# An edge-message kernel on one core: scatters eight groups behind throughout, and six slots for combined messages in place of three

## The chip, the cores and the metric

The kernel runs on one core of one Trainium2 chip. The metric is the device time of one execution in microseconds; the median of three runs of the kernel before is 1071.09 us.

## The reference

100,000 nodes with 64 features each, 25,000 edges with 32 features each. With `source, target = src, dst`:

```python
h = jnp.maximum(_layernorm(x, axis=-1), 0.0)
z = jnp.concatenate([h[source], h[target], edge_attr_32], axis=-1)
m = jax.nn.sigmoid(z @ W_f + b_f) * jax.nn.softplus(z @ W_s + b_s)
message = jax.ops.segment_sum(m, source, num_segments=100000)
mean = jnp.mean(message, axis=0)
var = jnp.mean((message - mean) ** 2, axis=0)
normed = (message - mean) * jax.lax.rsqrt(var + 1e-5) * gamma + beta
out = x + h + normed
```

## The kernel before

Stage one computes the messages. 128 edges are a tile, 4 tiles a group, and there are 49 groups (0 to 48, the last one is `LAST`). GpSimd gathers the rows of `x` for both ends of each edge by indirect DMA: 8 gathers of 128 rows for a group (line 584), into a ring of six groups. Beside each edge group a block of 16 x 128 nodes is normalised and kept as y = x + h. The engines work in steps (`step` in `vector`, `scalar` and `tensor`): in step s VectorE centres group s, TensorE transposes group s-1 and multiplies it with the weights (lines 1124, 1134 to 1138), and group s-3 is finished: VectorE forms the message, TensorE adds up the messages of edges in a group that have the same source (`combine`, lines 1164 and 1168, which signals `comb_done`), and ScalarE copies the combined messages out of PSUM (`copy_comb`, line 1036, which signals `comb_copied`). TensorE's next transposition of edge features (line 1117) waits for that copy.

The combined messages of a group stand in a slot of a ring of `COMB_SLOTS` = 3. GpSimd adds them to the table `msgs` in DRAM by four indirect DMAs with accumulation (`accumulate`, line 597, called the scatters here). A group's scatters wait for its copy, for its targets, and for the landing of the scatters of the group before (`accumulated`). Ahead of them GpSimd signals `slots_free`. For group n `copy_comb` waits for `slots_free` of n+1, and two are given at the start, so group n waits until the scatters of group n-2 have been let go.

GpSimd's order is written by hand. It gathers group n and then scatters group n-8. At n = 16, 24, 32 and 40 (`CATCH_UP`) another group's scatters stand between the first and the second half of the gathers, so that from n = 40 on GpSimd is four groups behind. Group 48 is gathered apart (`gather_last`, line 607) and is computed under the next stage. The last three groups (46 to 48, `LATE`) are not scattered in stage one: their combined messages are copied to the tile `late` and added later. Behind the scatters of group 45 GpSimd reads 12 times 128 rows of `msgs` for them (line 632, the late gathers).

Stage two scans `msgs` (25 blocks) for the sum of squares. SyncE issues its loads (line 1423) once all scatters of groups 0 to 45 have landed, the last node block is done (`y_done`, line 827) and the last transposition but one is over (`z_turned`). From the fourth block on they also wait for `cross_used`, which TensorE signals when matmuls for the joined group 47 are done (line 1150), and for the gathers of group 48. ScalarE's squares (line 1466) wait for the block and for TensorE's clearing of two PSUM banks behind those matmuls. Stage three writes out = y + normalised message.

Of the kernel before, what the change touches and what calls it, by code (L numbers as in the profile page):

```python
# [23 lines left out]
ALU = mybir.AluOpType  # L24
# [3 lines left out]
P = 128  # L28
NODES, EDGES, F, EF = 100000, 25000, 64, 32
EPS = 1e-5  # L30
TILES = 4
GATHERED = 2 * TILES
# [6 lines left out]
LAST = GROUPS - 1  # L39
# [9 lines left out]
G_SLOTS = 6  # L49
S_SLOTS = 2  # L50
E_SLOTS = 3
COMB_SLOTS = 3
LATE = 3
PRE = GROUPS - 1
EARLY = GROUPS - LATE
# [1 line left out]
SPILL = 19  # L57
KEPT_ROWS = (GROUPS - SPILL) * BULK
ACC_FIRST = 8
CATCH_UP = (16, 24, 32, 40)  # L60
ZERO_PARTS = 16
ZERO_EARLY = 5
ZERO_FIRST = 2
# [25 lines left out]
BANK_ROWS = 8  # L89
# [119 lines left out]
def build(nc, x, src, dst, ea, w_f, b_f, w_s, b_s, gamma, beta, out, msgs, y_spill):  # L209
# [7 lines left out]
    with ExitStack() as outer:  # L217
# [3 lines left out]
        def keep(name, shape, dt=F32):  # L221
            return outer.enter_context(nc.sbuf_tensor(name, shape, dt))

        at = Shared()
# [12 lines left out]
        at.late_out = keep("late_out", [P, LATE_TILES], I32)  # L237
        at.m_buf = keep("m_buf", [P, M_BUFS, S_BLK, F])
        at.m_last = keep("m_last", [P, BLOCKS[-1][1], F])
        at.sums = keep("sums", [P, 21 * F])  # L240
        at.ps_all = outer.enter_context(nc.psum_tensor("ps_all", [P, 2 * Y_ROWS, F], F32))

        at.accumulated = sem("accumulated")
# [55 lines left out]
def stage_one(nc, sem, keep, at, x, src, dst, ea, w_f, b_f, w_s, b_s, msgs, y_spill, src_rows,  # L299
# [3 lines left out]
    late_comb, late_msg, late_ids = at.late_comb, at.late_msg, at.late_ids  # L303
# [24 lines left out]
    ids = free_then(2, ALL_TILES, dt=I32)  # L328
# [4 lines left out]
    xg_last = free_last(GATHERED, F)  # L333
# [34 lines left out]
    before_scan = carver(at.sums[:, 0:BANK_ROWS * F])  # L368
    src_f = before_scan(ALL_TILES)
    msg = before_scan(TILES, F)  # L370
    comb = carver(at.sums[:, BANK_ROWS * F:20 * F])(COMB_SLOTS, TILES, F)
    sq = at.late[:, :, :]
    ids_turned = gate[:, :, :].rearrange("p (h t) f -> p h (t f)", h=2)
    upto = same[:, 0, :]
# [22 lines left out]
    def late_tiles(g):  # L397
        return slice((g.n - EARLY) * TILES, (g.n - EARLY + 1) * TILES)
# [2 lines left out]
        return late_msg[:, late_tiles(g), :] if g.late else msg[:, :, :]  # L401

    def comb_of(g):
        return late_comb[:, late_tiles(g), :] if g.late else comb[:, g.slot(COMB_SLOTS), :, :]

    def wait_slot(eng, g):

# [160 lines left out]
    def gpsimd(pool):  # L568
        pool.sem_inc(slots_free, COMB_SLOTS - 1)

        pool.memset(ident[:, :], 0.0).then_inc(masks_set, 1)
        pool.memset(upto[:, :], 1.0).then_inc(masks_set, 1)
        pool.wait_ge(masks_set, 2)
        pool.affine_select(out=ident[:, :], in_=ident[:, :], compare_op=ALU.not_equal, fill=1.0,
                           base=0, pattern=[[-1, P]], channel_multiplier=1).then_inc(masks_made, 1)
        pool.affine_select(out=upto[:, :], in_=upto[:, :], compare_op=ALU.is_ge, fill=0.0,
                           base=0, pattern=[[-1, P]], channel_multiplier=1).then_inc(masks_made, 1)

        def gather(n, tiles):
            if n >= G_SLOTS:  # L580
                pool.wait_ge(centred, n - G_SLOTS + 1)
            for j in tiles:
                for c in range(2):
                    pool.indirect_dma_start(  # L584
                        xg[:, n % G_SLOTS, 2 * j + c, :], None, x,
                        bass.IndirectOffsetOnAxis(ap=ids[:, c, n * TILES + j:n * TILES + j + 1], axis=0),
                    ).then_inc(gathered[n % G_SLOTS], 16)

        def accumulate(n):
            pool.wait_ge(comb_copied, n + 1)  # L590
            pool.wait_ge(target_done, n + 1)

            if n:
                pool.wait_ge(accumulated, 16 * TILES * n)
            pool.sem_inc(slots_free, 1)
            for j in range(TILES):
                pool.indirect_dma_start(  # L597
                    msgs, bass.IndirectOffsetOnAxis(ap=target[:, n % UNROLL, j:j + 1], axis=0),
                    comb[:, n % COMB_SLOTS, j, :], None, compute_op=ALU.add,
                ).then_inc(accumulated, 16)  # L600

        pool.wait_ge(ids_main, 32)
        behind = 0
        def gather_last(tiles):
            for j in tiles:
                for c in range(2):
                    pool.indirect_dma_start(
                        xg_last[:, 2 * j + c, :], None, x,
                        bass.IndirectOffsetOnAxis(ap=ids[:, c, LAST * TILES + j:LAST * TILES + j + 1], axis=0),
                    ).then_inc(last_gathered, 16)  # L610

        for n in range(PRE):
            gather(n, range(0, TILES // 2))
            if n in CATCH_UP:
                accumulate(behind)
                behind += 1
            gather(n, range(TILES // 2, TILES))
            if n == ACC_FIRST:
                pool.wait_ge(table_zeroed, 16 * (ZERO_PARTS + 2))
            if n >= ACC_FIRST:  # L620
                accumulate(behind)
                behind += 1
        pool.wait_ge(ids_rest, 64)
        for n in range(behind, EARLY):
            gather_last([n - behind])
            accumulate(n)
        gather_last(range(EARLY - behind, TILES))

        pool.wait_ge(late_listed, 1)
        pool.wait_ge(accumulated, 16 * TILES * EARLY)  # L630
        for t in range(LATE_TILES):
            pool.indirect_dma_start(
                was_read[:, t, :], None, msgs, bass.IndirectOffsetOnAxis(ap=late_ids[:, t:t + 1], axis=0),
            ).then_inc(late_read, 16)
# [1195 lines left out]
```

## Time and profile before

| | |
|---|---|
| median of 3 runs | 1071.09 us (1069.85 to 1071.23) |
| the profiled execution, from its first to its last instruction | 1087.2 us, 16.1 above that median |
| indirect DMAs in stage one, issued by GpSimd | 384 gathers, 184 scatters, 8 gathers of group 48, 12 late gathers |
| stage one, about | 0 to 860 us |
| scan, about | 860 to 950 us |
| output, about | 950 to 1087 us |

In a timeline each row is the start and the duration in us, the engine, the line, the operation and its tiles; in brackets stands how long the engine was idle before it, and what ended that. POOL is GpSimd, PE TensorE, PEld its weight loads, DVE VectorE, ACT ScalarE, and SPq SyncE's queue, which issues DMAs. In grouped rows "idle before" is the sum of such idle times.

### The profile page before, as it was taken

To read this page: it belongs to the slowest core of one execution; us is meant where nothing else is said; L and a number is where in the kernel's file an instruction comes from. 1 tells how busy PE (TensorE), PEld (TensorE's weight loads), DVE (VectorE), ACT (ScalarE), POOL (GpSimd) and SP (SyncE) were. 2 spreads that over 40 slices of the span, in tenths; PEclk is the share of its full clock that TensorE was granted. 3 is DMA by queue.
4 is the path that set the end of the run, shared out by engine and by line. 5 is a ranking of instruction groups with operands and counts; after the bars stand their busy time and mean duration, and the time that the engine had idled before them with its cause. 6 is when DMAs were issued, how large, how long until landed. Compare 5 with 4: busy or idle time off the path is not lost. (4 is left out here: it accounts for less than half of the span.)

```text
span 1087.2 us, 11011 instructions
## 1 busy us (share of the span) xinstructions
PE 579.7 (53%) x2442; PEld 406.6 (37%) x2442; DVE 742.1 (68%) x1551; ACT 536.9 (49%) x1185; POOL 735.4 (68%) x652
## 2 busy tenths in 40 slices
PE   0321754456553756664564556575636679844332
PEld 0121542335442534542352335454424479610000
DVE  3523766658766678757587666677566568789788
ACT  1131664556464656454565645664546556333332
POOL 7774777777878787777778777878787710650620
PEclk9855576765676565557666755655676579855555
DMA  7994443545443434434344334334333579589999
GB/s 280 416 402 151 111 124 75 123 94 123 104 120 77 125 59 79 85 56 83 62 83 78 86 53 86 62 78 82 63 76 58 153 290 410 195 254 414 416 404 387
DMA packets 88145, 176.02 MB, mean 162 GB/s; under 512 B 42561, under 2 KB 49285, under 8 KB 79663
## 3 DMA queue, kind: packets, MB, share of 16 engines
q1 hardware_dynamic: 34903, 111.46, 29.0%
q0 software_dynamic: 42880, 20.09, 16.5%
q10 hardware_dynamic: 10328, 44.12, 10.0%
q14 instruction: 26, 0.21, 0.1%
q8 instruction: 8, 0.13, 0.1%
HBM read 107.12 MB, written 68.50 MB: 162 GB/s over the span
## 5 line engine op out<-in xcount | busy, mean ns | idle before, releaser
L584 POOL DMA_INDIRECT m_buf<-in_x_dram,m_buf x384 | 368.4, 959 | 118.3 <-issue 111.6
L597 POOL DMA_INDIRECT msgs_dram<-sums,target x184 | 289.2, 1572 | 69.0 <-issue 56.0
L1164 PE MATMUL ps_all<-sums,m_last 128*128 128x64 f32 x920 | 152.2, 338 | 26.9 <-issue 23.7
L707 DVE TENSOR_REDUCE m_last<-late 128x24 f32<-128x1536 f32 (+1 forms) x49 | 85.3, 1741 | 113.8 <-ACT late L978 84.4
L1164 PEld LDWEIGHTS ps_all<-sums,m_last 128*128 128x128 f32 x920 | 145.9, 251 | 38.3 <-issue 35.4
L1117 PE MATMUL ps_all<-ident,m_last 128*128 128x128 f32 x49 | 21.2, 432 | 225.3 <-ACT sums L1036 212.0
L1138 PEld LDWEIGHTS ps_all<-m_buf 128*128 128x128 f32 x392 | 93.8, 328 | 50.0 <-issue 50.0
L1036 ACT ACTIVATE sums<-ps_all 128x256 f32<-128x256 f32 x46 | 17.6, 382 | 187.3 <-remote 187.3
L1027 ACT ACTIVATE m_last<-m_last,one_col 128x512 f32<-128x512 f32 x196 | 107.6, 550 | 1.6
L678 DVE SCALAR_TENSOR_TENSOR m_buf<-ps_all,m_buf 128x1024 f32<-128x1024 f32 x97 | 93.2, 960 | 19.3 <-remote 15.6
L827 DVE TENSOR_TENSOR y_kept<-ps_all,m_buf 128x256 f32 (+1 forms) x196 | 82.5, 422 | 26.6 <-remote 13.6
L1136 PE MATMUL ps_all<-m_buf 128*128 128x512 f32 x98 | 100.6, 1129 | 0.0
L1117 PEld LDWEIGHTS ps_all<-ident,m_last 128*128 128x128 f32 x49 | 8.9, 181 | 237.4 <-issue 237.0
L1019 ACT ACTIVATE m_last<-m_buf,m_last 128x512 f32<-128x512 f32 x196 | 93.5, 553 | 0.0
L1138 PE MATMUL ps_all<-m_buf 128*128 128x128 f32 x392 | 90.8, 411 | 0.0
L1457 ACT ACTIVATE ps_all<-y_kept 128x2048 f32<-128x2048 f32 (+3 forms) x33 | 47.0, 1432 | 80.0 <-DVE m_buf L1790 75.1
L837 DVE TENSOR_TENSOR sums<-m_buf 128x256 f32<-128x256 f32 x46 | 19.5, 423 | 95.0 <-ACT m_buf L994 86.6
L978 ACT ACTIVATE late<-m_buf 128x1536 f32<-128x1536 f32 (+1 forms) x49 | 71.5, 1459 | 25.2 <-issue 25.2
L1528 PE MATMUL ps_all<-shift_row,ones_b 3*128 3x512 bf16 x90 | 42.5, 619 | 75.1 <-ACT ps_all L1457 66.8
L809 DVE SCALAR_TENSOR_TENSOR ps_all<-m_buf,ps_all 128x512 f32<-128x512 f32 x98 | 67.7, 691 | 11.3 <-remote 8.6
L1124 PE MATMUL ps_all<-ident,m_buf 128*128 128x128 f32 x192 | 41.6, 356 | 59.2 <-issue 30.7
L687 DVE TENSOR_REDUCE ps_all<-m_buf 128x16 f32<-128x1024 f32 x49 | 59.9, 1222 | 14.0 <-DMA m_buf<-in_x_dram 12.9
(171 smaller groups left out, 1076.1 us busy)
## 6 DMA issues: line engine op xcount, KB each, us to landing
m_buf<-msgs_dram SPq DMA_DIRECT2D x38, 1024.0 KB, 8.4
m_buf<-in_x_dram SPq DMA_DIRECT2D x48, 512.0 KB
out_dram<-m_buf ACTq DMA_DIRECT2D x20, 1024.0 KB, 10.8
msgs_dram<-y_kept SPq DMA_DIRECT2D x11, 1536.0 KB
m_buf<-src_rows_dram SPq DMA_DIRECT2D x47, 256.0 KB
y_spill_dram<-y_kept ACTq DMA_DIRECT2D x19, 512.0 KB
y_kept<-y_spill_dram SPq DMA_DIRECT2D x8, 1024.0 KB, 14.8
msgs_dram<-y_kept ACTq DMA_DIRECT2D x5, 1536.0 KB
```

What stands on the lines that cost most here:

```text
L584: pool.indirect_dma_start(xg[:, n % G_SLOTS, 2 * j + c, :], None, x, bass.IndirectOffsetOnAxis(ap=ids[:, c, n * TILES + j:n * TILES + j + ...
L597: pool.indirect_dma_start(msgs, bass.IndirectOffsetOnAxis(ap=target[:, n % UNROLL, j:j + 1], axis=0), comb[:, n % COMB_SLOTS, j, :], None, ...
L678: return dve.scalar_tensor_tensor(out=xc[:, g.slot(2), rows, :], in0=row_sum[:, rows].unsqueeze(2).to_broadcast([P, n, F]), scalar=-1.0 / ...
L707: dve.tensor_reduce(row_ssq[:, rows], sq[:, rows, :], AX.X, ALU.add).then_inc(ssq_done, 1)
L809: dve.scalar_tensor_tensor(out=ps_h[:, :, :], in0=xc[:, g.slot(2), rows, :], scalar=0.0, in1=row_rstd[:, rows].unsqueeze(2).to_broadcast([ ...
L827: ins = dve.tensor_tensor(y_kept[:, bass.ds(row, n), :], ps_h[:, piece * n:(piece + 1) * n, :], xn[:, g.slot(SLOTS), of_x, :], ALU.add)
L978: act.activation(sq[:, rows, :], xc[:, g.slot(2), rows, :], ACT.Square).then_inc(squared, 1)
L1019: ins = act.activation(same_of(b, b, TILES), src_all[:, slot, b:TILES, :], ACT.Abs, scale=-1.0, bias=own[:, g.slot(UNROLL), b:b + 1])
L1027: ins = act.activation(same_of(b, b, TILES), same_of(b, b, TILES), ACT.Relu, scale=-1.0, bias=one_col[:, 0:1], accum_out=matches[:, b:b + 1])
L1136: pe.matmul(v[:, :, :], ea_t[:, :], w_e[:, :, :], start=False, stop=True, skip_group_check=True)
L1138: ins = pe.matmul(v[:, j, :], z_t[:, j, :], w_z[:, :], start=False, stop=True, skip_group_check=True)
L1164: pe.matmul(ps_c[:, j, :], same_of(b, j, j + 1)[:, 0, :], msg_of(g)[:, b, :], start=(b == 0 and not begun), stop=(b == j), skip_group_chec ...
```

## The change

GpSimd no longer catches up: it gathers group n whole and scatters group n-8, for all n up to 47. Then 6 groups (40 to 45) are left to scatter, where before 2 were (44 and 45). The 8 gathers of group 48 are spread ahead of these six, one or two each; before, two stood ahead of each of the two groups and four behind. The ring of combined messages has six slots; four lie in the tile `sums` and two in `m_buf`. With it `copy_comb` and the targets of group n wait until the scatters of group n-5 have been let go.

```diff
-COMB_SLOTS = 3
+COMB_SLOTS = 6
+COMB_FIRST = 4
-CATCH_UP = (16, 24, 32, 40)
...
-        at.sums = keep("sums", [P, 21 * F])
+        at.sums = keep("sums", [P, (BANK_ROWS + COMB_FIRST * TILES) * F])
...
-    comb = carver(at.sums[:, BANK_ROWS * F:20 * F])(COMB_SLOTS, TILES, F)
+    take_comb = carver(at.sums[:, BANK_ROWS * F:])
+    comb = [take_comb(TILES, F) if i < COMB_FIRST else free_then(TILES, F) for i in range(COMB_SLOTS)]
...
-        def gather_last(tiles):
-            for j in tiles:
-                for c in range(2):
-                    pool.indirect_dma_start(
-                        xg_last[:, 2 * j + c, :], None, x,
+        def gather_last(rows):
+            for row in rows:
+                j, c = divmod(row, 2)
+                pool.indirect_dma_start(
+                    xg_last[:, row, :], None, x,
...
         for n in range(PRE):
-            gather(n, range(0, TILES // 2))
-            if n in CATCH_UP:
-                accumulate(behind)
-                behind += 1
-            gather(n, range(TILES // 2, TILES))
+            gather(n, range(TILES))
             if n == ACC_FIRST:
                 pool.wait_ge(table_zeroed, 16 * (ZERO_PARTS + 2))
             if n >= ACC_FIRST:
                 accumulate(behind)
                 behind += 1
         pool.wait_ge(ids_rest, 64)
+        left = EARLY - behind
         for n in range(behind, EARLY):
-            gather_last([n - behind])
+            gather_last(range(GATHERED * (n - behind) // left, GATHERED * (n - behind + 1) // left))
             accumulate(n)
-        gather_last(range(EARLY - behind, TILES))
```

GpSimd's order about group 16, before. `m_buf<-in_x_dram` is a gather, `msgs_dram<-` a scatter, of the groups 7, 8, 9 and 10 in turn:

```order
L584 DMA m_buf<-in_x_dram,m_buf 128x64 x8
L597 DMA msgs_dram<-sums,target 101664x64 x4
L584 DMA m_buf<-in_x_dram,m_buf 128x64 x4
L597 DMA msgs_dram<-sums,target 101664x64 x4
L584 DMA m_buf<-in_x_dram,m_buf 128x64 x4
L597 DMA msgs_dram<-sums,target 101664x64 x4
```

The third to the sixth row hold the one group of gathers and two of scatters; in the changed kernel each eight gathers are followed by four scatters.

GpSimd's end of stage one, before: behind the eight gathers of group 47 the scatters are those of the groups 43, 44 and 45; `late_ids` are the late gathers.

```order
L584 DMA m_buf<-in_x_dram,m_buf 128x64 x8
L597 DMA msgs_dram<-sums,target 101664x64 x4
L607 DMA m_buf<-in_x_dram,m_buf 128x64 x2
L597 DMA msgs_dram<-sums,target 101664x64 x4
L607 DMA m_buf<-in_x_dram,m_buf 128x64 x2
L597 DMA msgs_dram<-sums,target 101664x64 x4
L607 DMA m_buf<-in_x_dram,m_buf 128x64 x4
L632 DMA m_buf<-msgs_dram,late_ids 128x64 x12
```

The same place in the changed kernel, from the scatters of group 39 behind the gathers of group 47 to the late gathers; a slot in `m_buf` is one of the two new ones.

```order
L598 DMA msgs_dram<-sums,target 101664x64 x4
L608 DMA m_buf<-in_x_dram,m_buf 128x64
L598 DMA msgs_dram<-m_buf,target 101664x64 x4
L608 DMA m_buf<-in_x_dram,m_buf 128x64
L598 DMA msgs_dram<-m_buf,target 101664x64 x4
L608 DMA m_buf<-in_x_dram,m_buf 128x64 x2
L598 DMA msgs_dram<-sums,target 101664x64 x4
L608 DMA m_buf<-in_x_dram,m_buf 128x64
L598 DMA msgs_dram<-sums,target 101664x64 x4
L608 DMA m_buf<-in_x_dram,m_buf 128x64
L598 DMA msgs_dram<-sums,target 101664x64 x4
L608 DMA m_buf<-in_x_dram,m_buf 128x64 x2
```

Behind the last of these rows stand the scatters of group 45 and the late gathers. Four groups of scatters have moved from between the gathers to behind all of them.

## Rows read from the trace of the kernel before

**Rows 1.** The page's first part: busy us and share of the span.

```profile
PE 579.7 (53%) x2442; PEld 406.6 (37%) x2442; DVE 742.1 (68%) x1551; ACT 536.9 (49%) x1185; POOL 735.4 (68%) x652
```

**Rows 2.** Grouped rows of GpSimd, 114 to 832 us: busy, mean ns, idle before.

```profile
L584 POOL DMA_INDIRECT m_buf<-in_x_dram,m_buf x312 | 300.1, 962 | 95.1 <-issue 89.9 <-DMA msgs_dram<-sums,target 5.2
L597 POOL DMA_INDIRECT msgs_dram<-sums,target x172 | 270.4, 1572 | 52.4 <-issue 52.4
```

**Rows 3.** ScalarE's waits, 120 to 832 us: total, times, longest.

```profile
ACT sums L1036 <- remote: 183.5, 35, 5.9
```

**Rows 4.** Timeline of ScalarE, the copies and one row ahead.

```profile
117.12 0.39 ACT L1036 ACTIVATE sums<-ps_all 128x256 f32<-128x256 f32 x1
...
237.22 0.38 ACT L1036 ACTIVATE sums<-ps_all 128x256 f32<-128x256 f32 x1 [5.79 <-remote]
...
249.06 0.36 ACT L1036 ACTIVATE sums<-ps_all 128x256 f32<-128x256 f32 x1
...
262.82 0.39 ACT L1036 ACTIVATE sums<-ps_all 128x256 f32<-128x256 f32 x1
...
814.13 0.38 ACT L1036 ACTIVATE sums<-ps_all 128x256 f32<-128x256 f32 x1 [5.75 <-remote]
...
825.27 0.72 ACT L1011 ACTIVATE m_buf<-m_buf,one_col 128x512 f32<-128x512 f32 x1
831.78 0.38 ACT L1036 ACTIVATE sums<-ps_all 128x256 f32<-128x256 f32 x1 [5.80 <-remote]
...
843.58 0.39 ACT L1036 ACTIVATE sums<-ps_all 128x256 f32<-128x256 f32 x1
...
856.07 0.36 ACT L1036 ACTIVATE late<-ps_all 128x256 f32<-128x256 f32 x1
```

**Rows 5.** Timeline of GpSimd: last and first transfers of some groups.

```profile
235.64 1.54 POOL L597 DMA_INDIRECT msgs_dram<-sums,target  x1 [0.30 <-issue]
...
806.98 1.61 POOL L597 DMA_INDIRECT msgs_dram<-sums,target  x1 [0.31 <-issue]
...
812.64 1.56 POOL L597 DMA_INDIRECT msgs_dram<-sums,target  x1 [0.30 <-issue]
...
823.36 0.94 POOL L584 DMA_INDIRECT m_buf<-in_x_dram,m_buf  x1 [0.30 <-issue]
...
830.27 1.54 POOL L597 DMA_INDIRECT msgs_dram<-sums,target  x1 [0.30 <-issue]
...
840.38 1.55 POOL L597 DMA_INDIRECT msgs_dram<-sums,target  x1 [0.30 <-issue]
...
845.00 1.61 POOL L597 DMA_INDIRECT msgs_dram<-sums,target  x1 [0.46 <-issue]
...
850.63 1.54 POOL L597 DMA_INDIRECT msgs_dram<-sums,target  x1 [0.30 <-issue]
...
871.53 0.94 POOL L632 DMA_INDIRECT m_buf<-msgs_dram,late_ids  x1 [0.30 <-issue]
```

**Rows 6.** Timeline of TensorE: the end of step 47's work.

```profile
822.67 0.65 PE L1168 MATMUL ps_all<-sums,ones 128*128 128x256 f32 x2
824.83 0.66 PE L1124 MATMUL ps_all<-ident,m_buf 128*128 128x128 f32 x4 [1.50 <-issue]
832.31 0.45 PE L1117 MATMUL ps_all<-ident,m_last 128*128 128x128 f32 x1 [6.83 <-ACT sums L1036]
```

**Rows 7.** Timeline of VectorE: the end of the last node block.

```profile
857.97 0.42 DVE L827 TENSOR_TENSOR y_kept<-ps_all,m_buf 128x256 f32<-128x256 f32 x1
```

**Rows 8.** Timeline of SyncE's queue: the scan's first loads.

```profile
858.46 1.39 SPq L1423 DMA_DIRECT2D m_buf<-msgs_dram  x3
...
875.77 0.90 SPq L1423 DMA_DIRECT2D m_buf<-msgs_dram  x2
```

**Rows 9.** Timeline of ScalarE: the scan's first squares.

```profile
875.46 1.12 ACT L1466 ACTIVATE ps_all<-m_buf 128x512 f32<-128x512 f32 x2 [11.89 <-remote]
```

**Rows 10.** DMA issues, 855 to 880 us: count, KB each, median us to landing.

```profile
m_buf<-msgs_dram SPq DMA_DIRECT2D x5, 1024.0 KB, 6.4
```

More of the change, by code:

```diff
@@ L403, in comb_of @@
     def comb_of(g):
-        return late_comb[:, late_tiles(g), :] if g.late else comb[:, g.slot(COMB_SLOTS), :, :]
+        return late_comb[:, late_tiles(g), :] if g.late else comb[g.slot(COMB_SLOTS)]
     def wait_slot(eng, g):
@@ L598, in accumulate @@
                     msgs, bass.IndirectOffsetOnAxis(ap=target[:, n % UNROLL, j:j + 1], axis=0),
-                    comb[:, n % COMB_SLOTS, j, :], None, compute_op=ALU.add,
+                    comb[n % COMB_SLOTS][:, j, :], None, compute_op=ALU.add,
                 ).then_inc(accumulated, 16)
@@ L603, in gpsimd @@
         behind = 0
-        def gather_last(tiles):
-            for j in tiles:
-                for c in range(2):
-                    pool.indirect_dma_start(
-                        xg_last[:, 2 * j + c, :], None, x,
-                        bass.IndirectOffsetOnAxis(ap=ids[:, c, LAST * TILES + j:LAST * TILES + j + 1], axis=0),
-                    ).then_inc(last_gathered, 16)
-        for n in range(PRE):
-            gather(n, range(0, TILES // 2))
-            if n in CATCH_UP:
-                accumulate(behind)
-                behind += 1
-            gather(n, range(TILES // 2, TILES))
+        def gather_last(rows):
[3 more added lines that the diff above has]
+                    xg_last[:, row, :], None, x,
+                    bass.IndirectOffsetOnAxis(ap=ids[:, c, LAST * TILES + j:LAST * TILES + j + 1], axis=0),
+                ).then_inc(last_gathered, 16)
+        for n in range(PRE):
+            gather(n, range(TILES))
             if n == ACC_FIRST:
```

## The prediction

> **What bounds the kernel now.** I read the busy shares first. GpSimd and VectorE are busy for 68% each, ScalarE and TensorE for about half [rows 1]; the shares name no bound, so the stages are read apart. In the edge stage (to about 860 us) the grouped rows of GpSimd for 114 to 832 us are to be read as a sum: 300.1 + 270.4 us of issuing and 95.1 + 52.4 us of gaps make 718.0 us, which is the window. The gaps are the 0.30 us ahead of each indirect transfer, put down to "issue" [rows 2, 5]. So GpSimd issues without a pause: a gather costs 0.96 + 0.30 us, a scatter 1.57 + 0.30 us, a group of 8 and 4 17.6 us. Neither kernel can make this stretch shorter than its transfers, and the change issues the same ones.
>
> Then I looked at who follows whom. ScalarE idles 183.5 us before 35 of its copies of a combined message (line 1036), at most 5.9 us each, and the releaser is given as "remote", none that the profile can show [rows 3]. The timeline of these copies has the pace [rows 4]. Group 46 is the first copy into the late tile (856.07), so group 44 is at 831.78 and group 43 at 814.13: 17.65 us apart, GpSimd's period. With group 8 at 237.22 and group 1 at 117.12 the pace is 17.2. After a catch-up it is faster: 237.22, 249.06, 262.82, steps of 11.8 and 13.8 us, and 11.8 again at 831.78 to 843.58, when the gathers are over.
>
> Beside GpSimd's timeline this is a lock [rows 5]: group 8 is copied at 237.22 as the scatters of group 7 end (237.18); group 43 at 814.13, those of 42 end at 814.20; group 44 at 831.78, those of 43 end at 831.81. The computing engines make one step for each group scattered, whether the scatters are eight groups behind the gathers or four. An inserted scatter group gave one more step.
>
> Is the lock the ring of three slots? By the waits, group 44 needs that the scatters of group 42 have been let go, which were issued from 806.98 [rows 5], 24.8 us before the copy. The slot was long free. What is late is TensorE: its matmuls of that group are recorded up to 823.32 and its transposes up to 825.49, ScalarE is free at 825.99, and all stand still until 831.78; TensorE's next begins at 832.31, released by that copy [rows 4, 6]. I have no cause for this. If the recorded ends were the whole truth, ScalarE would copy at 825.99, steps would take 11.9 us, and the first rival below would be the result. The copy's own time speaks against it. The Trainium skill (Perfetto Trace Analysis, section "Tensor Engine Instruction (MATMUL, LD_WEIGHTS)") says that a matmul's end is estimated by the profiler, not observed; by that rule TensorE may really have been busy or held up until 831.78, which leaves the forecast of 1091 where a reading by recorded ends gives 1068. The time of the copy agrees with the page.
>
> **The end of the stage.** The last gather of group 47 is issued by 824.30 [rows 5]. ScalarE copies group 44 in step 47, in which group 47 is centred: at 831.78 computing has caught up with the gathers, four steps closer than it started. The last node block is done at 858.39, and the scan's first loads go out at 858.46 [rows 7, 8], later than the last scatter's end (852.17 [rows 5]). So computing sets the start of the scan, not the scatters. Behind it the last of the twelve late gathers is issued by 872.48 [rows 5], and the first square of the scan waits until 875.46, again behind "remote" [rows 9], the fourth block's load until 875.77 [rows 8].
>
> **The change, part by part.** *Moved:* four groups of scatters, from between the gathers to behind them. Four scatters are 4 x 1.87 = 7.5 us, so the last gather is issued 30.0 us earlier, and the scatters of group 39 (in place of 43) end at 831.8 - 30.0 = 801.8. The first 16 groups are as before and cost nothing. *Computing:* if the lock holds, with the distance never reduced, the copy at 801.8 is group 40's; before, at 831.8, it is group 44's. Four more steps are to be made outside the lock. Their price lies between 11.8 us (the step after a catch-up, and 831.78 to 843.58) and 13.8 (the second such step). I take 12.8, the middle, as both occur in each pair: 801.8 + 51.2 = 853.0 for group 44, **21.2 us later** (17.2 to 25.2). From there the steps are as before, 26.6 us to the last node block: 879.6.
>
> *GpSimd's tail:* six scatter groups with 1 or 2 gathers between in place of two with 2. Each waits for the one before to land. Before, from the end of one group's last scatter (841.93) to the next start (845.00) is 3.07 us, with two gathers inside [rows 5]; one gather fills 1.6, so four such gaps cost 1.5 us each. In this case they are hidden, for a scatter group every 10.3 us (7.2 + 3.07) is faster than a step of 12.8: GpSimd will now wait for copies. Group 45 is copied at 853.0 + 11.8 = 864.8, its scatters start about 1.4 us later (843.58 to 845.00) and end at 873.4, still before 879.6. *The eight gathers of the last group* all come ahead of the last scatter, four more than before; SyncE needs them later and they lie in waits. The twelve late gathers follow the last landing, 3.07 us after 873.4, and take 12 x 1.25 - 0.30 = 14.7 us: 876.5 to 891.2, 18.7 us later than before. The first square came 2.98 us behind the last late gather (872.48 to 875.46), which would put it at 894.2, and 17.07 behind the node block, which puts it at 896.7: 18.7 to 21.2 later. I take **20**. *Three more slots* cost memory and no instruction; nobody waited for a slot, so they bring nothing. *Nothing moves in the scan or the last stage*, which hang on this start.
>
> Sum against the profiled execution: 1087.2 + 20 = 1107.2. Its span is 16.1 above the median of the plain runs, and I carry the difference over to them: 1071.1 + 20 = **1091**. Its own range is 1086 to 1097 (17.2 less 2.5 for the late gathers, and 25.2 with the 0.7 us that separate the runs).
>
> **The rivals.** *Computing is freed (faster).* If the slots do matter after all, computing catches up with the gathers and all of it, joined matmuls included, is over before the scatters are. Then GpSimd's chain decides: 801.8 + 6 x 10.27 = 863.4 for the last scatter, 11.2 later than before, loads at 863.4 + 3.07 = 866.5 at the latest (8.0 later), but nothing to wait for behind them. A load in this stretch lands 6.4 us after its issue [rows 10], so the first square is at 872.9, 2.6 earlier, and the fourth block's load 9 us earlier; the scan's loads are the tighter of the two, so I give it -3: **1068** (1065 to 1071). For it: three slots with eight groups behind bind by the code, if the copy is where the design has it. Against it: the 24.8 us of free slot, and that in the first phase, where the scatters are eight behind already, not one step in seven was won. It decides from the point where computing gains 1.6 steps (20 / 12.8) before the gathers end.
>
> *Computing is slowed further.* GpSimd's waits for landings between short runs hold up TensorE as the long runs do: steps of 17.6 in the tail, 4 x 17.6 = 70.4 in place of 30.0: +40, **1111**. Against it: at 831.78 to 843.58, with just two gathers and a scatter group, the step was 11.8.
>
> *It makes no difference.* Computing gains one or two of the four steps, for the lock is loose somewhere; then the node blocks end with the landing of the scatters, and the gain in preparation cancels the 8 us: **1071** (1069 to 1080).
>
> **How the numbers follow.** Lock holds 0.63; computing freed 0.22; between 0.10; slowed further 0.05. Likeliest: 1091. The range reaches from the freed case to the lock's upper bound: 1066 to 1097 leaves out the slowed case, a third of the freed one and some of the lock's. A measurement of this kernel tells 0.2% (2.1 us) from no change. Faster by more: most of the freed case and a little of the third, 0.21. Within: 0.07. Slower: 0.72.
>
> **What would show it.** In the profile after: copies of line 1036 still 17.6 us apart at 500 us with "remote" before them, and the scatters of group n-1 ending at each; the last gather issued at about 794, but the last node block not before 875; GpSimd with waits of 1 to 4 us for ScalarE's copies ahead of its last scatter groups; the scan's loads near 880 and the first square near 895. I am wrong if copies after the first ten come faster than 17.6 us each and then follow the gathers within a step; if the slots held ScalarE in a way that the waits don't show; or if the held-up TensorE depends on where messages lie in memory, which the ring moves.

## The result, and the profile after

The changed kernel takes 1077.75 us (median; 1077.39 to 1078.39) where the kernel before takes 1070.65 us. The ratio is 1.0067, with a 95% interval of 1.0052 to 1.0081: 0.7% or 7 us **slower**. The forecast was 1091 us; the direction was right, the size was off by almost a factor of three.

One of the five executions of the changed kernel was disturbed (1386 us) and is left out of these figures; the trace below is of a later execution of the same code, of 1078.7 us. The trace of before on which the prediction rests turned out to be unusual too: that execution was 16 us longer than the plain runs. A second trace of the kernel before has a span of 1069.4 us. The two new traces are compared here; "before" means the second trace, unless rows of the first are named.

**GpSimd between the gathers.** Grouped rows, 114 to 790 us, of the changed kernel:

```profile
L585 POOL DMA_INDIRECT m_buf<-in_x_dram,m_buf x310 | 296.8, 957 | 94.5 <-issue 82.0 <-DMA msgs_dram<-sums,target 4.6 <-ACT sums L1033 3.4
L598 POOL DMA_INDIRECT msgs_dram<-sums,target x105 | 164.6, 1568 | 32.0 <-issue 32.0
L598 POOL DMA_INDIRECT msgs_dram<-m_buf,target x48 | 75.4, 1572 | 14.6 <-issue 14.6
```

They answer to [rows 2]: 0.957 + 0.30 us for each gather, 1.57 + 0.30 for each scatter, no other idle time. This stretch runs as before.

**GpSimd's tail.** First the kernel before, then the changed one; each row is one transfer, and the first scatter of each group and its neighbours are shown. Before (groups 44 and 45, the rows of group 48, the late gathers):

```profile
824.54 1.54 POOL L597 DMA_INDIRECT msgs_dram<-sums,target  x1 [0.30 <-issue]
826.39 1.02 POOL L607 DMA_INDIRECT m_buf<-in_x_dram,m_buf  x1 [0.30 <-issue]
827.71 0.97 POOL L607 DMA_INDIRECT m_buf<-in_x_dram,m_buf  x1 [0.30 <-DMA msgs_dram<-sums,target]
828.99 1.61 POOL L597 DMA_INDIRECT msgs_dram<-sums,target  x1 [0.30 <-ACT sums L1036]
...
839.10 1.61 POOL L597 DMA_INDIRECT msgs_dram<-sums,target  x1 [0.30 <-issue]
...
844.73 1.74 POOL L597 DMA_INDIRECT msgs_dram<-sums,target  x1 [0.30 <-issue]
846.77 1.02 POOL L607 DMA_INDIRECT m_buf<-in_x_dram,m_buf  x1 [0.30 <-issue]
848.09 0.97 POOL L607 DMA_INDIRECT m_buf<-in_x_dram,m_buf  x1 [0.30 <-DMA msgs_dram<-sums,target]
849.37 0.94 POOL L607 DMA_INDIRECT m_buf<-in_x_dram,m_buf  x1 [0.30 <-issue]
850.62 0.94 POOL L607 DMA_INDIRECT m_buf<-in_x_dram,m_buf  x1 [0.30 <-issue]
851.87 0.94 POOL L632 DMA_INDIRECT m_buf<-msgs_dram,late_ids  x1 [0.30 <-issue]
```

After (from the end of group 39's scatters; the groups 40 to 45 start at 799.20, 808.67, 819.06, 828.85, 838.40 and 848.42):

```profile
795.28 1.55 POOL L598 DMA_INDIRECT msgs_dram<-sums,target  x1 [0.30 <-issue]
797.14 1.02 POOL L608 DMA_INDIRECT m_buf<-in_x_dram,m_buf  x1 [0.30 <-issue]
799.20 1.56 POOL L598 DMA_INDIRECT msgs_dram<-m_buf,target  x1 [1.04 <-DVE target L779]
...
808.67 1.56 POOL L598 DMA_INDIRECT msgs_dram<-m_buf,target  x1 [1.05 <-DMA msgs_dram<-m_buf,target]
...
828.85 1.56 POOL L598 DMA_INDIRECT msgs_dram<-sums,target  x1 [1.28 <-issue]
...
838.40 1.57 POOL L598 DMA_INDIRECT msgs_dram<-sums,target  x1 [1.13 <-DMA msgs_dram<-sums,target]
...
854.08 1.55 POOL L598 DMA_INDIRECT msgs_dram<-sums,target  x1 [0.30 <-issue]
857.99 1.02 POOL L629 DMA_INDIRECT m_buf<-msgs_dram,late_ids  x1 [2.37 <-DMA msgs_dram<-sums,target]
```

Read the bracket. Before, it is 0.30 us ahead of every row to the end: from the end of a group's last scatter to the next group's first there are 2.9 us with two gathers in them, while the landing and the restart need about 2.4 (after the change, the gaps that hold one gather are 2.4 to 2.6 us). The name in a bracket is the signal that came last before the start, and it is not always the cause: group 40's own targets and copy were long there at 799.20, and what ends there, as in the other gaps, is the landing of the group before (signalled at 798.34, the next scatter 0.86 later).

After, four of the six groups begin behind one gather and wait 0.74, 0.75, 0.98 and 0.83 us more than the usual 0.30 (3.3 us); and the late gathers wait 2.07 us more for the last landing, where before four gathers lay in it. That is 5.4 us in all in which GpSimd stands still, against none before. Beside it, four gathers of group 48 now stand ahead of the last scatters, not behind them (4 x 1.25 to 1.3 = 5.1 us).

The last scatter ends at 855.63 in place of 846.47, 9.2 us later. Of these, 2.0 lie ahead of the first scatter (103.56 against 101.57), which in this execution waited longer for the zeroed table (9.4 us over the usual gap, before 7.8); in the eight others of the table below that begin their scatters at the same place it starts at 101.2 to 101.8. So they belong to this execution and not to the change. From the first scatter's start to the last one's end the change costs 7.2 us (752.07 against 744.90), which is the loss of the plain runs. The parts are 5.1 + 3.3, less 0.4 for one wait that only before had and 1.0 by which the scatters took less to issue in all; that makes 7.0, and 0.2 is left.

**Computing and the scan.** Timelines: VectorE's last node block, SyncE's first loads of the scan, ScalarE's first square; before, and then after. They answer to [rows 7 to 9].

```profile
842.70 0.42 DVE L827 TENSOR_TENSOR y_kept<-ps_all,m_buf 128x256 f32<-128x256 f32 x1
...
848.04 1.61 SPq L1423 DMA_DIRECT2D m_buf<-msgs_dram  x3
...
854.80 1.12 ACT L1466 ACTIVATE ps_all<-m_buf 128x512 f32<-128x512 f32 x2 [6.51 <-DMA m_buf<-msgs_dram]
```

```profile
814.88 0.42 DVE L824 TENSOR_TENSOR y_kept<-ps_all,m_buf 128x256 f32<-128x256 f32 x1
...
857.22 1.28 SPq L1420 DMA_DIRECT2D m_buf<-msgs_dram  x3
...
863.93 1.12 ACT L1463 ACTIVATE ps_all<-m_buf 128x512 f32<-128x512 f32 x2 [43.45 <-DMA m_buf<-msgs_dram]
```

The last node block is done 28 us **earlier** after the change, and it no longer matters: ScalarE stands still for 43.45 us ahead of the first square, which waits for its block. In both kernels the first three loads go out as the last scatters land (848.03 and 857.21 by the trace's semaphore events), 9.2 us later after the change; the first square is 9.1 us later, the copy of group 48 8.7 us (905.84 and 914.52), the end of the span 7.6 (1069.4 and 1077.0). So 1.6 us come back behind the scan's first load. The fourth load, which waits for group 48's gathers, goes out 2.0 us behind the first after the change (859.25) and 10.3 us behind it before (858.34). Whether the 1.6 us come from there is not shown: in the usual traces the time from the first load to the end is 219.6 to 221.5 us, and does not follow this distance in each of them.

### The profile page after: what moved, and what is told of

Read it like the earlier page. It is cut to its first block, busy times and chain, and to the rows that moved or that the text cites. A ratio compares the mean times of both kernels' runs of the same rounds, so it can differ in the third digit from the quotient of the medians.

```text
span 1384.3 us, 11011 instructions
## 1 busy us (share of the span) xinstructions
PE 1239.6 (90%) x2442; PEld 920.5 (66%) x2442; DVE 741.6 (54%) x1551; ACT 536.6 (39%) x1185; POOL 731.2 (53%) x652
## 4 chain that ended last, share of the span: by engine, by line
PE 80%; DMA 7%; DVE 4%; SPq 4%; ACT 2%; issue 1%; ACTq 0%; DVEq 0%
PE ps_all L1161 26%; PE ps_all L1133 11%; PE ps_all L1135 11%; PE ps_all L1530 11%; PE ps_all L1165 6%; PE ps_all L1121 5%; DMA m_buf<-msgs_dram 4%; PE ps_all L1131 2%; PE ps_all L1525 2%; ACT m_buf L998 2%; PE ps_all L1197 2%; DMA out_dram<-m_buf 1%; PE ps_all L1114 1%; SPq L537 1%; DVE m_buf L1787 1%
## 5 line engine op out<-in xcount | busy, mean ns | idle before, releaser
L1161 PEld LDWEIGHTS ps_all<-sums,m_last 128*128 128x128 f32 x920 | 382.5, 593 | 10.8 <-issue 10.8
L1161 PE MATMUL ps_all<-sums,m_last 128*128 128x64 f32 x920 | 370.0, 557 | 10.1 <-ACT m_last L1024 10.1
L598 POOL DMA_INDIRECT msgs_dram<-sums,target x128 | 200.7, 1568 | 144.8 <-ACT sums L1033 104.9
L1135 PEld LDWEIGHTS ps_all<-m_buf 128*128 128x128 f32 x392 | 169.9, 478 | 99.9 <-issue 99.9
L1135 PE MATMUL ps_all<-m_buf 128*128 128x128 f32 x392 | 180.4, 741 | 0.0
L1133 PE MATMUL ps_all<-m_buf 128*128 128x512 f32 x98 | 168.7, 1882 | 0.0
L1530 PEld LDWEIGHTS ps_all<-m_buf 128*128 128x128 f32 x336 | 138.5, 590 | 10.9 <-issue 10.5
L1530 PE MATMUL ps_all<-m_buf 128*128 128x128 f32 x336 | 143.2, 647 | 0.0
L598 POOL DMA_INDIRECT msgs_dram<-m_buf,target x56 | 87.8, 1568 | 65.0 <-ACT m_buf L1033 51.6
L1121 PE MATMUL ps_all<-ident,m_buf 128*128 128x128 f32 x192 | 95.4, 733 | 11.1 <-DVE m_buf L794 11.1
L1165 PE MATMUL ps_all<-sums,ones 128*128 128x256 f32 x92 | 92.3, 1086 | 0.0
L1121 PEld LDWEIGHTS ps_all<-ident,m_buf 128*128 128x128 f32 x192 | 49.0, 256 | 55.9 <-issue 24.8
```

The lines of the kernel that those rows point to most:

```text
L598: pool.indirect_dma_start(msgs, bass.IndirectOffsetOnAxis(ap=target[:, n % UNROLL, j:j + 1], axis=0), comb[n % COMB_SLOTS][:, j, :], None, ...
L1121: ins = pe.transpose(ps_z[:, j, :], xc[:, g.slot(2), 2 * j:2 * j + 2, :].rearrange("p c f -> p (c f)"), ident[:, :])
L1133: pe.matmul(v[:, :, :], ea_t[:, :], w_e[:, :, :], start=False, stop=True, skip_group_check=True)
L1135: ins = pe.matmul(v[:, j, :], z_t[:, j, :], w_z[:, :], start=False, stop=True, skip_group_check=True)
L1161: pe.matmul(ps_c[:, j, :], same_of(b, j, j + 1)[:, 0, :], msg_of(g)[:, b, :], start=(b == 0 and not begun), stop=(b == j), skip_group_chec ...
L1165: ins = pe.matmul(ps_sum[:, 0:whole, :], ones[:, :], msg_of(g)[:, 0:whole, :], start=False, stop=True, skip_group_check=True)
```

## What held computing: the second trace of the kernel before

> The kernel before once more, for a second trace: the first one's execution was 16 us longer than the plain runs, and its first copy of a combined message was at 105 us, where the changed kernel and two of its variants have it at 73 to 74 us. If the lock of the prediction is the kernel's (copies at the ends of the scatters, remote releaser), it is here again, with an execution near 1087 us. If it belonged to that one execution, the first copy is at 73 to 75 us, the copies are released by slots (VectorE's write of target waits for GpSimd's release), and the execution is near 1070 us; what matters for the change is then when the last scatters end, which I expect near 847 us, 8 us before the changed kernel's.

Measured: 1070.44 us, the kernel before again (ratio 0.9992, 0.9983 to 1.0002). The first copy is at 73.81 us, not at 105.33. The copy of line 1036, its idle time, and the same for VectorE's write of the targets (total us, times):

```profile
L1036 ACT ACTIVATE sums<-ps_all x46: 362/383/385, 73.8 to 828.3; 128x256 f32<-128x256 f32 x46
...
  POOLq L595: 24.9, 20
```

```profile
L782 DVE TENSOR_TENSOR target<-moved,m_last x49: 161/163/217, 71.8 to 910.9; 128x4 int32<-128x4 f32 x49
its engine sat idle before it (us, times) until:
  POOLq L595: 76.0, 26
```

Where [rows 3] had "remote" 35 times, the releaser now has a name: GpSimd's queue at its release of a slot. VectorE writes a group's targets only once the slot is free, with everything else of its step queued behind it, and waits there longer than ScalarE does. This execution's last scatter ends at 846.47, as expected. At 495.94, 513.58 and 531.10 us the copies follow such releases. So in usual executions **the three slots are what holds computing** in the middle of the stage, as the code says. The first trace differs: VectorE's write of the targets never waits for a slot there, and group 20 is copied at 428.81, here at 398.03. TensorE's signal for a copy comes 8.4 us behind the recorded end of its matmul there (831.76, behind 823.33, for group 44), here at once (809.88, behind 809.86). Why is not known; in the eleven later traces shown in the table below the first copy is never later than 74.3 us. This trace also shows the scan waiting for other things: the last node block is done 4.9 us before the last landing, so the scatters start the scan's loads and computing does not.

The changed kernel's second trace was expected to tell slots from another lock:

> The changed kernel once more, for a trace in which TensorE runs at the clock of the kernel before. The lock of the prediction (copies of the combined messages follow the ends of the scatters, whatever the number of slots): copies 17.6 us apart at 500 us, the last gather near 794 us, last node block (y_kept) at 875 us or later, first square near 895 us; the measured +7 us would then have to come from a cheaper step than 12.8 us (four steps at some 9.5 us) or from a scan that gives time back. Rival, the slots were the lock: copies run ahead of the scatters by up to five groups, and the scatters' tail sets the scan: last scatter near 863 us, first square near 873 us, and the +7 us would have to lie in the scan.

Measured: 1077.57 us (ratio 1.0062, 1.0049 to 1.0076). Copies are 17.6 us apart at 500 us (500.11, 517.62, 535.26), but none waits for "remote":

```profile
DVE ps_all L695 <- DMA m_buf<-in_x_dram,m_buf: 93.4, 23, 4.4
...
DVE target L779 <- POOLq L596: 39.3, 24, 3.1
```

(VectorE's waits, 114 to 790 us: total, times, longest.) Computing runs at 13.7 us a step up to group 21, until it has caught up with the gathers; from there it takes the gathers' pace. VectorE still waits for a slot 24 times (39.3 us in all), as one is released once for each group of gathers. The rival's mechanism was the right one; its times, 863 for the last scatter and 873 for the first square, were 7 and 9 us too late (855.63 and 863.93).

## Experiments

In this table, by the traces: GpSimd's idle time beyond 0.30 us ahead of each indirect transfer, summed from 790 us to the last late gather; when the last scatter's issue ends; when the scan's first load goes out. The ratios are to the kernel before, run beside each kernel; as its time differs a little from set to set (1070.79 to 1071.88 us), kernels are compared by their ratios.

| kernel | idle, us | last scatter | first load | median us | ratio (95%) |
|---|---|---|---|---|---|
| ten groups first, six slots | 0.0 | 838.89 | 840.55 | 1064.31 | 0.9934 (0.9921 to 0.9947) |
| ten groups first, three slots | 0.0 | 839.05 | 840.70 | 1065.21 | 0.9936 (0.9923 to 0.9949) |
| six slots alone | 0.0 | 845.86 | 847.44 | 1070.85 | 0.9998 (0.9989 to 1.0007) |
| six slots, late catch-ups | 0.0 | 846.41 | 848.03 | 1069.79 | 0.9995 (0.9986 to 1.0004) |
| before | 0.0 | 846.47 | 848.04 | 1070.44 | 0.9992 (0.9983 to 1.0002) |
| six slots, rows 4 and 4 | 2.2 | 850.93 | 852.62 | 1074.87 | 1.0043 (1.0029 to 1.0056) |
| tail of four groups | 2.1 | 851.68 | 853.36 | 1076.02 | 1.0042 (1.0030 to 1.0054) |
| after, half the rows behind | 7.2 | 853.48 | 855.05 | 1078.01 | 1.0059 (1.0046 to 1.0072) |
| after | 5.4 | 855.63 | 857.22 | 1077.57 | 1.0062 (1.0049 to 1.0076) |
| after, three slots | 8.7 | 855.69 | 858.03 | 1080.89 | 1.0095 (1.0079 to 1.0110) |
| after, all rows ahead | 13.1 | 861.34 | 862.95 | 1084.61 | 1.0128 (1.0112 to 1.0143) |

Ordered by the first load, the kernels stand in the order of their ratios, but for neighbours that can't be told apart. The first load of "after" stands 2 us too late in this row by the late first scatter of its execution.

**Slots alone, and the change without its slots.** Six slots, catch-ups kept; in the first version the eight rows of group 48 are spread four and four ahead of the two last groups, in the second they stand as in the kernel before. The edits here are shown against the kernel before unless another is named, and the lines that lay out six slots, the same as in the change above, are left out:

```diff
-COMB_SLOTS = 3
+COMB_SLOTS = 6
+COMB_FIRST = 4
...
 CATCH_UP = (16, 24, 32, 40)
```

> The kernel before with six slots alone: the four catch-ups and the tail of two groups stay (the tail's rows of group 48 are spread four and four). Lock by something else than slots: nothing changes, 1071 us within 2 us, copies at the ends of the scatters as before. Slots were the lock: computing runs ahead between catch-ups and the time falls or the copies come earlier by 10 us or more; at most the scan starts a few us earlier, 1060 to 1070 us.

> Six slots alone, with the catch-ups and also the tail of the kernel before (rows of group 48: two, two, then four behind the last scatters). If it is only GpSimd's order that costs: 1071 us within 1.5 us, and the 4 us of the variant with spread rows came from the spreading. If six slots themselves cost (m_buf taken, scan loads later): 1074 to 1075 us again.

Measured 1074.87 and 1070.85 us. Six slots by themselves cost nothing and bring nothing, though computing runs ahead (group 20 is copied at 364.79 us, before at 398.03): the gathers hold it later, and group 44 is copied at 810.01 against 810.79. What cost 4 us in the first version is the spreading: four rows moved ahead of the last scatters, and nothing left to fill the last landing (2.2 us).

The change with the three slots of before and the tail of the changed kernel:

```diff
 COMB_SLOTS = 3
...
-CATCH_UP = (16, 24, 32, 40)
+CATCH_UP = ()
...
```

> The change without its ring: no catch-ups, six groups of scatters behind the last gather, three slots as before. Lock by something else than slots: as the changed kernel, 1078 us within 2 us. Slots matter once the scatters trail by eight: clearly slower than the changed kernel, near the 1091 us of the prediction.

Measured 1080.89 us, ratio 1.0095: 3 us slower than the changed kernel (the intervals do not overlap), between the two expectations. In the tail GpSimd stands still for longer ahead of two groups, and one load of SyncE stands beside the second:

```profile
827.38 1.56 POOL L597 DMA_INDIRECT msgs_dram<-sums,target  x1 [2.25 <-issue]
...
834.07 0.35 SPq L519 DMA_DIRECT2D m_buf<-src_rows_dram  x1
...
838.47 1.56 POOL L597 DMA_INDIRECT msgs_dram<-sums,target  x1 [2.67 <-DVE target L782]
```

The second bracket names VectorE's write of targets, but that write (at 837.64) is of group 45. The scatters that begin at 838.47 are those of group 44, whose targets were written at 823.89 and whose copy was made at 825.89; group 43's were ready earlier still, at 812.14. By the semaphore events both waits end with a late landing: 2.5 us behind the last scatter (826.33 behind 823.81) and 3.1 (837.62 behind 834.48), where the changed kernel's landings in the tail take 1.5 to 1.6. So GpSimd does not wait for computing here, and the wait of 1 to 4 us for ScalarE's copies, which the prediction had for the changed kernel, is in neither. What differs beside the two landings is that with three slots computing is later (group 44 is copied at 825.89, in the changed kernel at 781.54) and SyncE still loads its input: six loads are issued at 820.3 to 822.5 us and one of 256 KB at 834.07; in the changed kernel none is issued from 809 to 857 us. That these loads hold the landings up fits the figures of the last section but was not tested apart; a like load that SyncE issues at 836.22 in the kernel before, just as group 44's last scatter ends, does no harm (landing 1.6 us). The last landing is late too (858.02, 2.3 us), with no load beside it; that stays open.

So six slots are worth 3 us beside the long tail and nothing without it.

**The distance without the long tail.** Six slots; GpSimd is eight groups behind up to group 43, and catches up inside the last gathers:

```diff
...
-CATCH_UP = (16, 24, 32, 40)
+CATCH_UP = (44, 45, 46, 47)
```

> Six slots, and GpSimd stays eight groups behind until group 44, then catches up inside the gathers of groups 44 to 47 (one group of scatters each between four gathers), with the tail of the kernel before. Theory, the loss is landings that nothing covers in a tail of six groups: as six slots with the old catch-ups, whatever that gives (1071 to 1075 us). Rival, being eight groups behind for most of the stage costs by itself: as the changed kernel, 1078 us. The lock of the prediction gives the old time too, near 1071.

Measured 1069.79 us, ratio 0.9995. With six slots, being eight groups behind for all groups up to 43 costs nothing. Only where the last four groups are scattered counts: between gathers, or in a row behind them.

**The dose.** Two of the four catch-ups, six slots: a tail of four groups, with two rows ahead of each and none behind.

```diff
...
-CATCH_UP = (16, 24, 32, 40)
+CATCH_UP = (32, 40)
```

> Six slots, catch-ups at groups 32 and 40 alone: four groups of scatters behind the last gather, two rows of group 48 ahead of each, none behind. GpSimd's chain: four rows move ahead of the last scatters (5.1 us), four gaps of about 2.9 us hold two rows each at 2.5 (0.8 us more than in the kernel before), so the last scatter ends near 852.4 us, 3 us ahead of the changed kernel's, and the time is 1074 to 1076 us. Rival, each catch-up left out costs the same, whatever the rows: 1074.3 us (half of 7); rival, the rows ahead of the last scatters are all of it and the time is that of the changed kernel, 1077 to 1078 us.

Measured 1076.02 us, ratio 1.0042, which is 1075.3 us against the usual 1070.8; the last scatter ends at 851.68, 0.7 us before the expected time. With two rows in each gap no scatter group waits; the cost is the four rows moved ahead and the last landing, which is bare. One price for each catch-up would give half of the changed kernel's loss, a ratio of 1.0031 to 1.0033; that lies in the interval, so this run alone does not exclude that rival. The next two do: there no catch-up is changed, and the time moves.

**Where the rows stand.** All eight rows ahead of the six groups; the edit is to the changed kernel:

```diff
-            gather_last(range(GATHERED * (n - behind) // left, GATHERED * (n - behind + 1) // left))
+            if n == behind:
+                gather_last(range(GATHERED))
             accumulate(n)
```

> The changed kernel with all eight gathers of group 48 ahead of the six groups of scatters, not spread among them. GpSimd's chain: seven rows no longer lie in waits for landings, some 1.25 us each less what the first gap covers, so the last scatter ends 5 to 8 us later (861 to 864 us) but computing can end 50 us earlier and leaves the scan free of it. Theory, the last landing sets the end: 1081 to 1085 us. Rival, what is left of computing beside the scan sets the end: 1065 to 1075 us.

Measured 1084.61 us, ratio 1.0128, as the landings have it. GpSimd's timeline shows a whole landing in each gap, five times in the tail and once ahead of the late gathers:

```profile
840.65 1.54 POOL L598 DMA_INDIRECT msgs_dram<-sums,target  x1 [0.30 <-issue]
844.70 1.54 POOL L598 DMA_INDIRECT msgs_dram<-sums,target  x1 [2.50 <-DMA msgs_dram<-sums,target]
...
854.26 1.54 POOL L598 DMA_INDIRECT msgs_dram<-sums,target  x1 [2.48 <-DMA msgs_dram<-sums,target]
...
863.72 1.02 POOL L630 DMA_INDIRECT m_buf<-msgs_dram,late_ids  x1 [2.38 <-DMA msgs_dram<-sums,target]
```

The issued transfers are the same in number and kind; 7.7 us more of standing still than in the changed kernel, less the 2.0 us by which this execution's first scatter is earlier, make the last scatter 5.7 us later; the time is 7 us longer. That computing could end 50 us earlier did not come true: groups 46, 47 and 48 are copied at 815.12, 876.89 and 919.95, in the changed kernel at 813.75, 871.27 and 914.52. So this run speaks for the landings, but it did not give computing the head start that the rival needed.

Four rows behind the last scatters again, the others ahead of groups 41, 42, 44 and 45; again the edit is to the changed kernel:

```diff
-            gather_last(range(GATHERED * (n - behind) // left, GATHERED * (n - behind + 1) // left))
+            gather_last(range(TILES * (n - behind) // left, TILES * (n - behind + 1) // left))
             accumulate(n)
+        gather_last(range(TILES, GATHERED))
```

> The changed kernel with four of the eight rows of group 48 behind the last scatters, as in the kernel before, and the other four at 0, 1, 1, 0, 1, 1 ahead of the six groups. Theory, the landings: a gap is 2.4 us with one row in it and not shorter with none, so the last scatter ends only 1 to 2 us earlier (854 us), the late gathers 1 to 2 us later, and the time is 1077 to 1080 us. Rival, the rows moved ahead of the last scatters are the cost and not the landings: four rows of 1.25 us come back, 1073 us.

Measured 1078.01 us. The four rows do come out from ahead of the last scatter, but it ends only 2.1 us earlier (0.7 of which were there at the end of group 39's scatters, ahead of the tail), and the late gathers end 0.8 us later (873.60, after 872.76): the gaps are no shorter for holding fewer rows.

```profile
827.30 1.54 POOL L598 DMA_INDIRECT msgs_dram<-sums,target  x1 [2.42 <-DMA msgs_dram<-sums,target]
...
836.81 1.57 POOL L598 DMA_INDIRECT msgs_dram<-sums,target  x1 [1.09 <-DMA msgs_dram<-sums,target]
```

2.42 us without a row, 1.09 beside a row of 1.02 + 0.30: the gap is 2.4 us either way. So rows moved ahead and bare landings are one cost, not two: with six groups behind the gathers there is too little other work for six landings, wherever the eight rows stand.

**If GpSimd's chain is the bound, idle time at its start must count as much as at its end.** In the second trace of before GpSimd waits 8.1 us for the zeroed table:

```profile
92.50 0.94 POOL L584 DMA_INDIRECT m_buf<-in_x_dram,m_buf  x1 [0.30 <-issue]
101.57 1.61 POOL L597 DMA_INDIRECT msgs_dram<-sums,target  x1 [8.12 <-DMA msgs_dram<-y_kept]
```

The eight gathers of one more group take 10.0 us and fill it, with one more catch-up to keep the tail at two groups. The edit is the same with six slots and with three:

```diff
...
-ACC_FIRST = 8
-CATCH_UP = (16, 24, 32, 40)
+ACC_FIRST = 9
+CATCH_UP = (16, 22, 28, 34, 40)
```

> Six slots, GpSimd begins its scatters after ten groups of gathers in place of nine (the tenth fills the 8.1 us in which it waits for the zeroed table at 93 to 101 us), with five catch-ups, so that the tail is the two groups of the kernel before. Theory, GpSimd's chain of issues and uncovered waits sets the end: all of it comes 7.5 us earlier, last scatter ends near 839 us, 1062 to 1065 us. Rival, computing in the last steps sets the end: it hangs on the last gather too, so it would also be earlier, but if it does not follow, 1069 to 1071 us.

> The same with the three slots of the kernel before. Theory: slots matter only where the scatters trail by eight or more at the end of the stage; with the distance brought back to four the time is that of six slots, within 2 us. Rival, nine groups of distance with three slots hold computing back for good: 3 us or more above the six-slot kernel.

Measured 1064.31 us with six slots and 1065.21 with three, ratios 0.9934 and 0.9936: 7 us **faster than before**, and by the ratios 14 us faster than the changed kernel. With six slots:

```profile
103.00 0.94 POOL L586 DMA_INDIRECT m_buf<-in_x_dram,m_buf  x1 [0.30 <-issue]
104.25 1.61 POOL L599 DMA_INDIRECT msgs_dram<-sums,target  x1 [0.30 <-issue]
```

```profile
840.55 1.66 SPq L1425 DMA_DIRECT2D m_buf<-msgs_dram  x3
```

The wait is gone and the loads start 7.5 us earlier. These two are the best of all kernels run and can't be told apart, so no more slots are needed than in the kernel before.

## Why the prediction was right in its sign and wrong in its size

*GpSimd issues without a pause; a gather and a scatter cost 1.26 and 1.87 us.* Right; the last gather of group 47 ends at 789.3, expected at 794. Of the 5.0 us, 3.0 are the late first scatter of the execution that was read (106.54, here 103.56) and some 1.5 its slower gathers (962 against 957 ns, 310 times).

*The lock of computing to the ends of the scatters, by something other than the slots.* Wrong for the kernel, true only of the one execution that was read. "The slot was long free" was right of that execution, and VectorE's write of the targets shows no wait for a slot in it either; in the second trace that write waits 76.0 us for slots. So looking at VectorE would not have helped: the reading fits its trace, and the trace is unlike the eleven later ones. The 16 us over the plain runs had given notice of that. The page of the Trainium skill cited there (Perfetto Trace Analysis, on estimated ends of matmuls) was no help in deciding: the new traces name GpSimd's release. In the first trace the signal came 8.4 us behind the recorded end; whether the matmul really lasted so long no run here shows.

*"So computing sets the start of the scan, not the scatters."* **This is the step that failed**, and with it the term of +21.2 us. The forecast had the last node block at 879.6 and the first square near 895; they are at 815 and 863.9. There were no four steps at 12.8 us to be made up: with six slots the node blocks were done 42 us before the scatters landed, and even in the kernel before the last block was done before the landing (843.1 against 848.0).

*"In this case they are hidden"*, of the landings in the tail. Nothing hid them. The prediction had them at 1.5 us for each gap with one gather and then put them at nothing behind steps of 12.8 us, which were not there; measured were 0.7 to 1.0 for each of the four, and 2.1 ahead of the late gathers. The page DMA: Bandwidth & Descriptors of the Trainium skill (Anatomy of one DMA, SWDGE path) has about 2.0 us of fixed cost for each DMA issued by GpSimd, most of it in the receipt of the last write. The trace is of that order: 1.58 us from the end of the last scatter's issue (855.63) to its landing (857.21), and bare gaps of 2.4 to 2.5 us between groups. The prediction's own measure from the first trace, 3.07 us, held two gathers and did not show how much of it was landing.

*The first rival.* Its mechanism was the right one (computing freed, GpSimd's chain decides). It had the last scatter 11.2 us later (measured 9.2) and the loads 8.0 us later (9.2). It still came out at 1068, because it set this against a first square at 875.46, which was late by 20.7 us in that execution alone (854.80 in the second). Against a usual execution its own +8 would have given 1079.

*Carrying the 16.1 us over as a constant.* This hid the trouble. They were no fixed overhead: that trace is 5.0 us late at the first scatter, 5.7 at the end of the last and 20.7 at the first square, which is the very place on which the sum rested.

*Three more slots bring nothing, for nobody waited for a slot.* For the slots alone the outcome is right (0.9998), the reason is not: usual executions wait for slots, but this wait is not on the path that sets the end. With the tail of six groups they are worth 3 us.

What stays open: what delayed TensorE's signals in the first trace; by what 1.6 us come back behind the scan's first load; and whether SyncE's loads are what makes two landings late with three slots.

## What to carry to other kernels

If the profiled execution is over 1% longer than the plain runs, take a second one before arguing from a wait without a named releaser. And where a releaser is named, check that it is of the group that is waited for: twice here the name was of a signal that came by chance at the same time. Where an engine issues dependent DMAs in groups, count the landings that have no other issue beside them: what can fill them (here gathers, two to a landing) must be kept for the end of the queue, and a lag that costs nothing in the middle costs a bare landing for each group that is left over. And once an engine's chain is found to be the bound, look for its idle time everywhere, at its start too.

## What the runs showed of the hardware

How long small indirect DMAs take to land goes with what is in flight beside them. Behind the changed kernel's last two rows of group 48 (issued by 848.1 us, with no large load in flight) the landing came 1.5 us later, at 849.57. In the kernel before they are issued by 851.6, beside three loads of 1024 KB issued from 848.04, and land at 857.91, 6.4 us later. The scan's fourth load waits for them (858.34); half the rows behind in the changed kernel gave 6.2 us again (858.6 to 864.84).

The scatters show the same. In the second trace of before, the last signal of a group's landing comes 1.5 to 1.7 us behind the end of the group's issue in the 19 groups beside which the other queues move under 10 KB, and 1.5 to 5.4 us behind it, 3.1 in the median, in the 24 groups beside which they move over 60 KB (counted from 0.5 us ahead of that end to 1.6 behind it). Between gathers this costs nothing, for 5 to 10 us of gathers stand there; in the tail it is waited for.
